# Target loop of a graph network: transposes by pairs of fields, products tile by tile, ranks in two halves

## What is computed

```python
def _L0_gnn_ref(x, edge_index, edge_attr, W1, b1, gamma, beta, W2, b2):
    row, col = (edge_index[0], edge_index[1])
    ef = jnp.concatenate([x[row], x[col], edge_attr], axis=-1)
    h = ef @ W1 + b1
    mu = jnp.mean(h, axis=0)
    var = jnp.mean((h - mu) ** 2, axis=0)
    h = (h - mu) * jax.lax.rsqrt(var + BN_EPS) * gamma + beta
    h = jax.nn.relu(h)
    msgs = h @ W2 + b2
    sums = jax.ops.segment_sum(msgs, row, num_segments=n_nodes)
    ...
    return out + x
...
x = _layernorm(x + _L0_gnn_ref(x, edge_index, edge_attr_2, ...), axis=-1)
x = _layernorm(x + _L1_gnn_ref(x, ..., edge_index), axis=-1)
```

## Time and profile before

| what | value |
|---|---|
| median of 3 runs | 3951.27 us (3950.59 to 3957.7) |
| the profiled execution's own time | 3951.36 us |
| its span | 3949.5 us |
| PE busy | 3769.3 us (95%) |
| DVE busy | 2573.1 us (65%) |
| ACT busy | 1395.4 us (35%) |
| target loop | from 96 us (first key) to 1198.24 + 6.30 us (last L896) |

### The profile page before, as it was taken

How to read it: one execution, slowest core, us unless ns; L and a number is a source line. 1 busy time by engine, 2 the same in 40 slices (tenths; PEclk the granted TensorE clock), 3 DMA queues, 4 the chain that set the end, 5 groups by cost and what they waited for, 6 DMA issues and landing times.

```text
span 3949.5 us, 104146 instructions
## 1 busy us (share of the span) xinstructions
PE 3769.3 (95%) x42510; PEld 2695.9 (68%) x42510; DVE 2573.1 (65%) x3609; ACT 1395.4 (35%) x3527; POOL 85.1 (2%) x53
## 2 busy tenths in 40 slices
PE   4699999999998799999999999997999999999999
PEld 3488888888887688887888888884444444454444
DVE  7999999999993688888888888875111111111222
ACT  5355555545543355554555455545000000000000
POOL 0000000000000000000000000000000000000000
PEclk9899999999998899999999999999999999999999
DMA  7123223232233733333333333334666566656664
GB/s 238 51 83 99 84 87 93 84 96 88 81 98 140 122 126 129 133 122 125 124 132 131 124 126 129 126 114 144 196 196 197 188 199 196 196 189 207 211 204 139
DMA packets 397700, 547.34 MB, mean 139 GB/s; under 512 B 175743, under 2 KB 335240, under 8 KB 390440
## 3 DMA queue, kind: packets, MB, share of 16 engines
q1 hardware_dynamic: 390856, 537.51, 42.9%
q10 hardware_dynamic: 6624, 6.42, 0.5%
HBM read 434.34 MB, written 109.53 MB: 138 GB/s over the span
## 4 chain that ended last, share of the span: by engine, by line
PE 91%; DVE 4%; SPq 2%; ACT 1%; issue 1%; DMA 1%; ACTq 0%; DVEq 0%
PE py L1579 29%; PE pY L835 10%; PE ph L1298 10%; PE ph L1296 10%; PE pSum L1312 10%; PE pbk L896 8%; PE pA L822 3%; PE ph L1291 3%; PE pX L827 2%; PE pS L826 1%; PE pbk L873 1%; PE ptr L881 1%; DVE prod_raw L1120 1%; PE pg L1567 1%; SPq L1245 1%
## 5 line engine op out<-in xcount | busy, mean ns | idle before, releaser
L1579 PE MATMUL py<-ring_raw,p 128*128 128x512 bf16 (+1 forms) x3822 | 783.4, 367 | 18.0 <-DVE dummy L1739 16.1
L1298 PE MATMUL ph<-q,prod_raw 128*128 128x128 bf16 x7056 | 781.7, 220 | 0.8 <-issue 0.8
L1296 PE MATMUL ph<-p,prod_raw 128*128 (+1 forms) x7056 | 780.9, 220 | 0.0
L1579 PEld LDWEIGHTS py<-ring_raw,p 128*128 128x128 bf16 x3822 | 362.2, 98 | 430.9 <-DVE dummy L1739 16.5
L1296 PEld LDWEIGHTS ph<-p,prod_raw 128*128 128x128 bf16 x7056 | 518.6, 98 | 110.9 <-issue 2.7
L1347 ACT ACTIVATE x<-ph 128x512 bf16<-128x512 f32 x588 | 351.2, 597 | 668.0 <-PE ph L1298 664.7
L1439 DVE SCALAR_TENSOR_TENSOR ring_raw<-ph,x 128x512 f32<-128x512 f32 x588 | 404.3, 688 | 182.0 <-ACT x L1347 170.8
L1312 PE MATMUL pSum<-x,ring_raw 128*128 128x384 bf16 x2401 | 499.6, 327 | 8.9 <-DVE x L1444 8.9
L835 PE MATMUL pY<-p,ring_raw 128*128 128x128 bf16 x7203 | 501.0, 219 | 0.2 <-issue 0.2
L1298 PEld LDWEIGHTS ph<-q,prod_raw 128*128 128x128 bf16 x7056 | 495.8, 98 | 0.0
L1755 DVE TENSOR_TENSOR yt<-py,dinv_row 128x512 f32<-128x512 f32 (+1 forms) x39 | 25.8, 661 | 697.1 <-PE py L1579 697.1
(11 more groups left out here) (322 smaller groups left out, 3906.0 us busy)
## 6 DMA issues: line engine op xcount, KB each, us to landing
ring_raw<-at_dram SPq DMA_DIRECT2D x252, 896.0 KB, 4.8
prod_raw<-lrow_dram SPq DMA_DIRECT2D x147, 768.0 KB, 4.2
at_dram<-ring_raw SPq DMA_DIRECT2D x49, 1568.0 KB, 5.6
prod_raw<-lrow_dram SPq DMA_DIRECT2D x49, 832.0 KB, 4.3
arow_dram<-x SPq DMA_DIRECT2D x147, 73.5 KB
x<-arow_dram SPq DMA_DIRECT2D x147, 54.0 KB
q<-q_dram SPq DMA_DIRECT2D x1, 4704.0 KB, 25.6
ring_raw<-at_dram SPq DMA_DIRECT2D x21, 224.0 KB, 2.5
```

The costliest lines, as they stand in the source:

```text
L1296: nc.tensor.matmul(bank[:, k * P:(k + 1) * P], T[q][:, 0, at:at + P], p_b[:, :, m3, :].rearrange("p a d -> p (a d)"), start=False, stop=False)
L1298: last = nc.tensor.matmul(bank[:, k * P:(k + 1) * P], T[q][:, 1, at:at + P], q3[:, c, m3, :], start=False, stop=m3 == 2 and k == w - 1)
L1579: last = nc.tensor.matmul(py[par][:, 0:w], g3[c % 2][:, 7 * i + m, k, :], ring[i][:, 0:w // P, m, :], start=i == m == k == 0, stop=i == m ...
```

## The change

Three things change in the target loop, all of them in how the same numbers are laid out and counted.

1. Two neighbouring fields of `cells` (2 x 50 columns) are the weights of one transpose. Four transposes write 100 partitions x 512 numbers instead of eight that write 49 x 1024. SP stores each half of the partitions by DMAs of its own: eight in a step instead of four.
2. `prod` has the tile of edges outside and the fields inside, so that an edge's 8 x 49 numbers are one run with a step of 2.
3. The 34 edges of a partition are ranked in two halves, 18 and 16. An edge of the second half comes after all first halves of its cell. So the counts have two parts: the first half's as before, and the second's, which sums the first halves of all partitions (`onesb`) and the second halves of the lower ones (`upper`). `known` is compared only within a half.

```diff
-SEL = B + TPB
+HALF = 9
+SEL = B + 2 * HALF
...
-                prod = prod_raw[:].rearrange("p (f g k u) -> p f g k u", f=8, g=TG, u=2)
+                prod = prod_raw[:].rearrange("p (g f k u) -> p g f k u", f=8, g=TG, u=2)
...
-                            sp.dma_start(lrow_dram[:, :, one, :].rearrange("b f c s -> b f (c s)"), rows_t[1 - par][0:B, 0:2, :]).then_inc(rows_out[1 - par], 16)
-                            for j in range(3):
-                                sp.dma_start(arow_dram[:, 6 * j:6 * j + 6, one, :].rearrange("b f c s -> b f (c s)"), rows_t[1 - par][0:B, 2:8, :]).then_inc(rows_out[1 - par], 16)
+                            for h in range(2):
+                                own = rows_t[1 - par][BW * h:BW * h + B]
+                                sp.dma_start(lrow_dram[:, h:h + 1, one, :].rearrange("b f c s -> b f (c s)"), own[:, 0:1, :]).then_inc(rows_out[1 - par], 16)
+                                for k in range(3):
+                                    sp.dma_start(arow_dram[:, 6 * k + h:6 * k + 6:2, one, :].rearrange("b f c s -> b f (c s)"), own[:, 1:4, :]).then_inc(rows_out[1 - par], 16)
...
                             for i in range(TPB):
-                                last = nc.tensor.matmul(pbk[:, BASE:BASE + B], upper[:], hot_p[:, i // 2, :, i % 2], start=i == 0, stop=i == TPB - 1)
+                                later, hot = i >= 2 * HALF, hot_p[:, i // 2, :, i % 2]
+                                if not later:
+                                    nc.tensor.matmul(pbk[:, BASE:BASE + B], upper[:], hot, start=i == 0, stop=False)
+                                last = nc.tensor.matmul(pbk[:, BASE + B:BASE + 2 * B], upper[:] if later else onesb[:], hot, start=False, stop=i == TPB - 1)
...
-                            for f in range(8):
-                                last = nc.tensor.transpose(ptr[0:B, f * P:(f + 1) * P], cells[1 - par][:, f, 0:B], identb[:])
+                            for j in range(4):
+                                last = nc.tensor.transpose(ptr[0:2 * BW, j * P:(j + 1) * P], cells[1 - par][:, 2 * j:2 * j + 2, :].rearrange("p f b -> p (f b)"), identb[:])
...
-                                last = nc.tensor.matmul(pbk[:, 0:8 * B], orank[:, i // 2, :, i % 2], prod[:, :, i // 2, :, i % 2], start=i == 0, stop=i == TPB - 1)
+                                last = nc.tensor.matmul(pbk[:, 0:8 * B], orank[:, i // 2, :, i % 2], prod[:, i // 2, :, :, i % 2].rearrange("p f k -> p (f k)"), start=i == 0, stop=i == TPB - 1)
...
-                            for g in range(TG):
-                                n = 2 * g + 1
-                                nc.scalar.activation(known[:, g, 0:n, :], key[:, 0:n].unsqueeze(2).to_broadcast([P, n, 2]), ACT.Copy)
+                            for h, (lo, hi) in enumerate(((0, HALF), (HALF, TG))):
+                                for g in range(hi - lo):
+                                    n = 2 * g + 1
+                                    nc.scalar.activation(known[h][:, g, 0:n, :], key[:, 2 * lo:2 * lo + n].unsqueeze(2).to_broadcast([P, n, 2]), ACT.Copy)
...
-                            nc.scalar.activation(rows_t[1 - par][0:B, :, :].rearrange("p f s -> p (f s)"), ptr[0:B, :], ACT.Copy).then_inc(S["rows_ready"], 1)
+                            nc.scalar.activation(rows_t[1 - par][0:2 * BW, :, :].rearrange("p j s -> p (j s)"), ptr[0:2 * BW, 0:4 * P], ACT.Copy).then_inc(S["rows_ready"], 1)
...
-                            return V.tensor_tensor(prod[:, f, :, :, :], hot_p, rec[u][:, 2 + f, :].rearrange("p (g u) -> p g u", u=2).unsqueeze(2).to_broadcast(dims), ALU.mult)
+                            return V.tensor_tensor(prod[:, :, f, :, :], hot_p, rec[u][:, 2 + f, :].rearrange("p (g u) -> p g u", u=2).unsqueeze(2).to_broadcast(dims), ALU.mult)
```

More of the change, by code:

```diff
@@ L663, in build @@
                 rec = [in_q3.take(NF * TPB).rearrange("p (f t) -> p f t", f=NF) for u in range(2)]
-                prod = prod_raw[:].rearrange("p (f g k u) -> p f g k u", f=8, g=TG, u=2)
+                prod = prod_raw[:].rearrange("p (g f k u) -> p g f k u", f=8, g=TG, u=2)
                 in_x1 = Carve(x1_f[:, X1_FREE:].bitcast(BF16))
-                known = in_x1.take(TG * TPB * 2).rearrange("p (g t u) -> p g t u", g=TG, t=TPB)
+                known_raw = in_x1.take((HALF * 2 * HALF + (TG - HALF) * (TPB - 2 * HALF)) * 2)
+                known = [known_raw[:, 0:HALF * 2 * HALF * 2].rearrange("p (g t u) -> p g t u", g=HALF, t=2 * HALF), known_raw[:, HALF * 2 * HALF * 2:].rearrange("p (g t u) -> p g t u", g=TG - HALF, t=TPB - 2 * HALF)]
                 cells = [in_x1.take(9 * BW).rearrange("p (f b) -> p f b", f=9) for u in range(2)]
-                rows_t = [in_x1.take(8 * P).rearrange("p (f s) -> p f s", f=8) for u in range(2)]
+                rows_t = [in_x1.take(8 * P)[:, 0:4 * P].rearrange("p (j s) -> p j s", j=4) for u in range(2)]
                 in_x1f = Carve(x1_f[:, X1_FREE + in_x1.at // 2:])
@@ L768, in sp_1 @@
                     for u in range(2):
-                        sp.wait_ge(rows_out[u], 64 * ((B + 1 - u) // 2))
+                        sp.wait_ge(rows_out[u], 128 * ((B + 1 - u) // 2))
                         sp.wait_ge(a_out[u], 16 * ((B + 1 - u) // 2))
@@ L1010, in dve_1 @@
                     link(V.memset(lo_all[:, :, B:BW], 0.0))
-                    link(V.memset(known, -1.0))
+                    link(V.memset(known_raw, -1.0))
                     for u in range(2):
@@ L1086, in dve_1 @@
                     dve.wait_ge(proj_out[1], 32 * 6)
+                    link(V.memset(sel[:, :, B + TPB - 2 * HALF:SEL, :], 0.0))
                     for u in range(4):
@@ L1140, in step @@
                             dve.wait_ge(S["based"], s + 1)
-                            selected = mark(V.tensor_tensor(sel[:, :, 0:B, :], hot_p, base_2[:].unsqueeze(1).to_broadcast([P, TG, B, 2]), ALU.mult))
+                            V.tensor_tensor(sel[:, 0:HALF, 0:B, :], hot_p[:, 0:HALF], base_2[:, 0:1, :, :].to_broadcast([P, HALF, B, 2]), ALU.mult)
+                            selected = mark(V.tensor_tensor(sel[:, HALF:TG, 0:B, :], hot_p[:, HALF:TG], base_2[:, 1:2, :, :].to_broadcast([P, TG - HALF, B, 2]), ALU.mult))
                             after(counted)
                             after(selected)
-                            first = mark(V.tensor_tensor(sel[:, :, 0:41, :], sel[:, :, 0:41, :], sel[:, :, 42:83, :], ALU.add))
+                            first = mark(V.tensor_tensor(sel[:, :, 0:33, :], sel[:, :, 0:33, :], sel[:, :, 34:67, :], ALU.add))
                             after(first)
-                            second = mark(V.tensor_tensor(sel[:, :, 0:21, :], sel[:, :, 0:21, :], sel[:, :, 21:42, :], ALU.add))
+                            second = mark(V.tensor_tensor(sel[:, :, 0:17, :], sel[:, :, 0:17, :], sel[:, :, 17:34, :], ALU.add))
                             after(second)
-                            third = mark(V.tensor_tensor(sel[:, :, 0:10, :], sel[:, :, 0:10, :], sel[:, :, 11:21, :], ALU.add))
+                            third = mark(V.tensor_tensor(sel[:, :, 0:8, :], sel[:, :, 0:8, :], sel[:, :, 9:17, :], ALU.add))
                             after(third)
                             with nc.allow_low_precision(reason="whole numbers, and a rank up to 128 is exact"):
-                                ranked = mark(V.tensor_reduce(out=rank[:].rearrange("p (g u) -> p g u", u=2), in_=sel[:, :, 0:11, :].rearrange("p g k u -> p g u k"), op=ALU.add, axis=AX))
+                                ranked = mark(V.tensor_reduce(out=rank[:].rearrange("p (g u) -> p g u", u=2), in_=sel[:, :, 0:9, :].rearrange("p g k u -> p g u k"), op=ALU.add, axis=AX))
                             after(ranked)
```

14 lines of the change are left out of this document (8 added, 6 removed).

## The result

The changed kernel takes 3930.31 us (median of 5 runs, 3927.97 to 3932.56), beside 3950.59 us (5 runs, 3949.77 to 3957.7) for the kernel before in the same comparison. The ratio is 0.9946 (95% interval 0.9931 to 0.996): faster by 0.5%, some 21 us, where 13.3 us were forecast. The sign was right, the size was not, and two terms in the sum turned out to be wrong in opposite directions.

A forecast was written before the change was run, and what follows sets the result against it. PE was taken to bound from step 3 on, DVE the first three steps. Savings of 10.9 us in steps 3 to 48 and 1.4 + 1.0 in the first three make 13.3, from 3951.27 to 3938 us; range 3930 to 3953.

The forecast's parts named there:

- DVE's cover: DVE in steps 3 to 48: 0.48 us a step lighter, two steps 44.04 us against PE's 44.71, so PE still bounds.
- Products: PE's L896 matmuls, read in one run: pace from 185 to 168.5 ns, saving 0.568 us a step, 26.1 us in 46.
- Rival A: Products' matmuls: half the gain, the moving side's step costs and grows with columns, pace 173.6 ns, 3946.6 us; chance 0.15.
- Transposes: PE's L881, four with 100 weight columns for eight with 49: saves 0.143 us a step, 6.6 us in 46.
- change of kind at the end: Time from the last transpose to the group of cells behind it, beyond the steady 56 ns pace; no saving counted.
- Counts: PE's L873, 52 small matmuls instead of 34 at 26.4 ns: costs 0.475 us a step, 21.9 us in 46.
- Net: PE's saving in steps 3 to 48: 0.568 + 0.143 - 0.475 = 0.236 us a step, 10.9 us in 46.
- The first steps: First three loop steps, hanging on DVE: 1.4 us from its lighter work, 1.0 us from products' matmuls at the high clock.
- What was to cost nothing: ScalarE's copies (transposed rows from 1.01 to about 0.60 us) and SP's four more DMAs, about 2 us, hidden by waits.
- B: Products' matmuls: breaks between runs are free, the long stepped read costs 185 ns; slower, 3965 us; chance 0.12.
- C: DVE writes scattered products more slowly and becomes the bound; at +100 ns each, 3962 us; chance 0.05.
- D: PE's small matmuls are dear, 30 ns each of 52, with no gain from the transposes; 3953 us; chance 0.08.

The follow-up runs named there:

- the bursts: The changed kernel with bursts of 34 matmuls added in step 48, differing in moving side and weights; run once with a profile, its time not compared.

## Why the prediction was right and wrong

**The bound.** Right: PE bounded and still does. DVE's cover was counted as 0.48 us a step and its least step as 22.02, measured 22.06. Taken away (without the halves), DVE bounds at 22.53, as the prediction's condition says.

**Products, 0.568 us a step.** Too much: 34 x (185.1-173.3) = 0.401. (The 16.7 ns of the sum are 185 less 168.3, not less the 168.5 that it says it takes; that is a third of a microsecond in all.) The failed step is the reading of the 2.5 ns in L822 and L1312: I gave it to the weights' step, and so took 168.5 ns for a moving side with a step. Rival A's mechanism, that the step costs and grows with the columns, is what the bursts show, and its 173.6 ns is the measured pace. Too large by 0.167 us a step, 7.7 us in 46.

**Transposes, 0.143.** Too little: 0.41. Two steps failed. The load of 100 columns lasts 125 ns and not 158, and costs nothing at a pace of 56 ns, so the 3 x 27 ns subtracted don't exist. The 158 came from a line between a load in bf16 and one in f32; in bf16 the loads of 128 columns in the trace of before last only 97. By the Trainium skill's columns/1.2 ns ("TensorE: Matmul & The Clock Gate", LDWEIGHTS) the pace would be 83, by the estimate in the prediction, and the trace of the changed kernel doesn't show it. And the "change of kind at the end" in the earlier trace rows was seen and left in the sum as unchanged. It is 96 ns behind the transposes, with another 90 in front of them hidden in the counts' row. Gone are 90 + 225 + 96 = 411 ns: too small by 0.27 us a step, 12.3 us in 46, the largest miss.

**Counts, 0.475.** Right: from the first to the last count a step takes 1.330 us instead of 0.874 (medians of 38 steps), so 0.456. The pace is 26 ns with one kind of weights or two.

**Net.** 0.40 + 0.41 - 0.456, and 0.01 between the products and L861, give 0.37 us, which is what the measured step fell by. Forecast was 0.236. That the sum came within 8 us is partly luck: the products' error of 7.7 us and the transposes' of 12.3 have opposite signs. Rival A's time, 3946.6, was wrong although its mechanism held, since it shared the transposes' term.

**The first steps, 2.4 us.** About right. Step 3's first L903 comes 3.19 us earlier, 0.57 of which lie before the first key. The products of steps 0 to 2, in three windows of L903 alone that hold them whole, as in the earlier trace rows:

```profile
sum 26.10, PE 23.98 PEld 11.51; mean PE 7.99 PEld 3.84
```

24.90 less 23.98 is 0.92, and 1.0 was forecast. Counting the share at the high clock was right: in either kernel 41 of the 99 distances between these matmuls are longer than 200 ns, most of them 327, and at 327 the new layout gains nothing, as forecast. But the size is luck. The other 58 distances shrink by 11.8 ns each, which is 0.68 us; the rest lies in the few distances at which a step's products start or the clock rises.

**What was to cost nothing** did. ScalarE's copy of the transposed rows takes 0.58 us, and SP has issued its eight DMAs by 1013.92 and then waits for the diagonal until 1024.54:

```profile
1009.54 0.58 ACT L980 ACTIVATE x<-ptr 100x512 bf16<-100x512 bf16 x1
...
1012.71 1.21 SPq L764 DMA_DIRECT2D arow_dram<-x  x3
1024.54 0.36 SPq L768 DMA_DIRECT2D at_dram<-ring_raw  x1
```

**Rivals.** B is out (173, not 185), C too (1022 ns a product in both layouts), D as well (26 ns a count).

## What to carry to other kernels

Where two engines fill a loop, write down each one's sum and take the longer for every version. A part that costs time alone, as the halves do, can be what lets two others pay. In this kernel matmuls whose weights have 64 columns or fewer cost about 0.1 us at each end where they stand among wider ones; pack two of them, or widen the weights beyond 64, and look for that gap in front of a group, where a row's length hides it. Count TensorE's moving side in pieces of 16 bytes that it touches, not in columns, as soon as it is read with a step or in short runs.

## What the runs showed of the hardware that I had not expected

- A change between weights of 64 columns or fewer and of 65 or more costs 93 to 96 ns at the first matmul (149 to 152 instead of 56) and 10 to 24 at the second, in either direction, in bf16. In f32, padding 7 columns to 128 took 91 and 98 ns away. One column more in the loop saved 0.22 us a step.
- A stepped moving side costs 1.76 ns for each 16 bytes it touches, and 1 to 2 ns a matmul: 173, 261, 347 and 690 ns for 392 columns with steps of 2, 3, 4 and 8. The weights' step is free (173.3 and 172.7; 165.8 and 165.8).
- A load of 100 bf16 columns takes 125 ns and hides behind a matmul pace of 56.
- Open: L1312's 165 ns for 384 side-by-side columns where a burst has 162.5, and the 0.65 ns for the odd end of each side-by-side run.
